# A four-batch attention, gated-FFN and scan kernel: layer-norm statistics of batches 1 to 3 in the pipeline fill, third loop iteration written out

## What is computed

```
x = x + attention(layernorm(x))     # 16 heads, low-rank q and kv, rotary part, causal softmax
x = x + ffn(layernorm(x))           # gate and up from a 16-entry table, silu, down
x = x + scan_layer(layernorm(x))    # projections, softplus decay, linear recurrence over tokens
x = x + ffn(layernorm(x))

def layernorm(x, eps=1e-5):
    m = mean(x, -1); v = var(x, -1)
    return (x - m) / sqrt(v + eps)
```

## Time and profile before

| | |
|---|---|
| median of 3 runs | 880.52 us (873.76 to 881.05) |
| the profiled execution | 879.84 us |
| its span, first to last instruction | 877.7 us |
| mean granted TensorE clock | 0.973 |
| busy: PE, DVE, ACT, POOL | 88%, 77%, 71%, 57% |

### The profile page before, as it was taken

The page is one execution under the profiler, slowest core; times in us unless marked ns, Lnnn a source line. Parts: engine busy times, 40 slices in busy tenths (PEclk is TensorE's granted clock), DMA queues, the critical chain, the costliest instruction groups (busy, mean ns, idle before and its releaser), DMA issues.

```text
span 877.7 us, 16980 instructions
## 1 busy us (share of the span) xinstructions
PE 771.6 (88%) x4556; PEld 657.8 (75%) x4556; DVE 673.6 (77%) x2210; ACT 624.7 (71%) x1532; POOL 502.4 (57%) x545
## 2 busy tenths in 40 slices
PE   4768989898887988977889899998798999999998
PEld 4656777777766877866777779876686887887887
DVE  3776898787789877879987789886666678777643
ACT  3457978898786988887889889998434666656232
POOL 1599999999999999999999999830000000000000
PEclk9788999999999999999999999999999999999999
DMA  9700000000000000000000010000000000000000
GB/s 238 250 1 1 1 1 2 1 2 1 4 2 1 1 1 2 1 5 2 0 1 1 2 38 1 1 1 1 1 1 1 1 1 1 1 1 24 26 25 24
DMA packets 15402, 14.78 MB, mean 17 GB/s; under 512 B 5793, under 2 KB 14433, under 8 KB 15041
## 3 DMA queue, kind: packets, MB, share of 16 engines
q1 hardware_dynamic: 13792, 11.41, 4.6%
q0 software_dynamic: 624, 2.12, 0.7%
q10 hardware_dynamic: 880, 0.04, 0.1%
HBM read 11.46 MB, written 2.10 MB: 15 GB/s over the span
## 4 chain that ended last, share of the span: by engine, by line
PE 50%; DVE 17%; issue 16%; ACT 15%; DVEq 1%; DMA 0%; ACTq 0%; SPq 0%
PE bank L562 10%; PE bank L564 10%; PE bank L563 10%; ACT prob L764 6%; PE bank L1371 4%; ACT prob L746 3%; ACT pt_hi L773 2%; DVE o_b L1067 2%; DVE bias_m L1020 2%; PE bank L1398 2%; PE bank L1400 2%; PE bank L1385 1%; PE bank L1388 1%; DVE q_tok L1034 1%; PE bank L1336 1%
## 5 line engine op out<-in xcount | busy, mean ns | idle before, releaser
L696 POOL TENSOR_SCALAR hot<-idx_gu,lut 128x256 f32<-128x256 bf16 x165 | 191.0, 1158 | 16.7
L746 ACT ACTIVATE prob<-bank,bias_m 128x128 f32<-128x128 f32 (+3 forms) x256 | 136.6, 534 | 27.6 <-DVE bias_m L1020 26.8
L1020 DVE CUSTOM_DVE_ANT_0 bank<-bank,mask 128x128 f32<-128x128 f32 (+3 forms) x256 | 126.3, 494 | 31.8 <-issue 30.7
L764 ACT ACTIVATE prob<-prob,rden 128x128 f32<-128x128 f32 (+3 forms) x256 | 128.0, 564 | 10.4 <-DVE rden L1052 6.2
L1061 DVE TENSOR_TENSOR pt_lo<-bank,pt_hi 128x512 fp32r<-128x512 f32 x160 | 109.3, 683 | 32.2 <-ACT pt_hi L773 32.1
L701 POOL TENSOR_TENSOR w_gu<-w_gu,hot 128x256 f32<-128x256 f32 x165 | 122.0, 739 | 13.8
L1371 PE MATMUL bank<-ident,prob 128*128 128x128 f32 x640 | 101.0, 281 | 24.6 <-ACT prob L764 17.3
L773 ACT CAST pt_hi<-bank 128x512 fp32r<-128x512 f32 x160 | 94.6, 591 | 20.0 <-PE bank L1371 13.9
L1371 PEld LDWEIGHTS bank<-ident,prob 128*128 128x128 f32 x640 | 74.3, 142 | 43.4 <-ACT prob L764 25.4
L696 POOL TENSOR_SCALAR hot<-idx_dn,lut 128x256 f32<-128x256 bf16 (+1 forms) x90 | 96.3, 1071 | 9.1
L562 PE MATMUL bank<-kt_hi,qt_hi 128*128 128x128 f32 (+3 forms) x256 | 89.6, 350 | 10.1 <-ACT kt_hi L739 4.3
(11 more groups left out here) (198 smaller groups left out, 2149.1 us busy)
## 6 DMA issues: line engine op xcount, KB each, us to landing
x<-in_L_attn_a_x_dram SPq DMA_DIRECT2D x4, 512.0 KB, 7.5
wo_nat<-in_L_attn_a_wo_dram SPq DMA_DIRECT2D x1, 2048.0 KB, 13.1
out_dram<-x SPq DMA_DIRECT2D x16, 128.0 KB, 1.7
wqu<-in_L_attn_a_wq_up_dram SPq DMA_DIRECT2D x2, 768.0 KB, 7.6
wqr<-in_L_attn_a_wq_rope_dram SPq DMA_DIRECT2D x4, 192.0 KB, 8.0
raw_dn<-in_L_ffn_down_idx_dram POOLq DMA_DIRECT2D x1, 688.0 KB, 10.4
raw_gu<-in_L_ffn_gate_idx_dram POOLq DMA_DIRECT2D x1, 640.0 KB, 7.7
raw_gu<-in_L_ffn_up_idx_dram POOLq DMA_DIRECT2D x1, 640.0 KB, 8.3
```

The lines of the kernel that those rows point to most:

```text
L696: nc.gpsimd.tensor_scalar(dst, idx[:, c:c + n], float(v), lut[:, v:v + 1], ALU.is_equal, ALU.mult).then_inc(lut_hot, 1)
L746: nc.scalar.activation(prob[:, n % 2, h, 0:w], bank[2 + h % 2][:, 0:w], ACT.Exp, bias=bias_m[:, n % 2, h:h + 1], scale=-1.0, accum_out=den ...
L764: nc.scalar.activation(prob[:, n % 2, h, 0:w], prob[:, n % 2, h, 0:w], ACT.Copy, scale=rden[:, n % 2, h:h + 1]).then_inc(norm_a, 1)
L1020: nc.vector.tensor_tensor_reduce(out=bank[2 + h % 2][:, 0:w], in0=bank[2 + h % 2][:, 0:w], in1=mask[:, TB * P - w:TB * P], scale=1.0, scal ...
```

## The change

Three things are done. (1) A new function at_stats_of computes statistics and reciprocal roots for a range of batches into tiles of their own (at_stats, at_mv, at_r); it is called for batch 0 at the start and for batches 1 to 3 at once behind fill slot 1, where only batch 1 was worked on. (2) In the loop body DVE's slots 8 and 9 keep only the four normalisations (at_norm), in the same four gaps of slot 9 as before. (3) The loop has 2 iterations; the third (b = 2) is written out on PE, ACT and DVE, and its layer norm of batch 0 for the FFN stays in slots 8 and 9 as it was. The wait for the loads of batches 2 and 3 moves ahead to fill slot 1.

```diff
+        def at_stats_of(b0, b1):
+            e, tiles = nc.vector, slice(b0 * TB, b1 * TB)
+            for t in range(b0 * TB, b1 * TB):
+                e.bn_stats(at_stats[:, t, :], x[:, t, :]).then_inc(at_bn, 1)
+            e.wait_ge(at_bn, b1 * TB)
+            settle(2 * G)
+            for t in range(b0 * TB, b1 * TB):
+                e.bn_aggr(at_mv[:, t, :], at_stats[:, t, :]).then_inc(at_agg, 1)
+            e.wait_ge(at_agg, b1 * TB)
+            c0 = 1 if b0 == 0 else RSQRT + 2
+            e.tensor_scalar(at_v[:, tiles], at_mv[:, tiles, 1], LN_EPS, None, ALU.add).then_inc(at_ref, 1)
+            for k in range(RSQRT):
+                rsqrt_step(k, at_ref, c0, at_v[:, tiles], at_r[:, tiles], at_t[:, tiles])
+
+        def at_norm(p, t):
+            e = nc.vector
+            free_after(e, xt_mm, 2 * p)
+            if t == 0:
+                e.wait_ge(at_ref, (RSQRT + 1) * (1 if isinstance(p, int) and p == 0 else 2))
+
+            def rows(m):
+                return m[:, bass.ds(p * TB + t, 1)]
+            e.tensor_scalar(xn[:, t, :], rows(x).rearrange("p a d -> p (a d)"), rows(at_mv)[:, :, 0], rows(at_r),
+                            ALU.subtract, ALU.mult).then_inc(ln_norm, 1)
+
         def ln_step(k, p, xb):
             e = nc.vector
 
             def rows(t):
                 return x[:, bass.ds(xb * TB + t, 1), :].rearrange("p a d -> p (a d)")
-            c0 = (RSQRT + 1) * p + 1
+            q = p - BATCH
+            c0 = (RSQRT + 1) * q + 1
             if k < TB:
                 e.bn_stats(stats[:, k, :], rows(k)).then_inc(ln_stats, 1)
             elif k == TB:
-                e.wait_ge(ln_stats, p * TB + TB)
+                e.wait_ge(ln_stats, q * TB + TB)
                 e.wait_ge(ln_norm, p * TB)
                 settle(2 * G)
                 for t in range(TB):
                     e.bn_aggr(mv[:, t, :], stats[:, t, :]).then_inc(ln_aggr, 1)
-                e.wait_ge(ln_aggr, p * TB + TB)
+                e.wait_ge(ln_aggr, q * TB + TB)
                 e.tensor_scalar(ln_v[:, :], mv[:, :, 1], LN_EPS, None, ALU.add).then_inc(ln_ref, 1)
             elif k <= TB + RSQRT:
                 rsqrt_step(k - TB - 1, ln_ref, c0, ln_v[:, :], ln_r[:, :], ln_t[:, :])
@@ -519,10 +551,6 @@
                 e.wait_ge(xt_mm, 2 * p)
                 e.tensor_scalar(xn[:, t, :], rows(t), mv[:, t, 0:1], ln_r[:, t:t + 1],
                                 ALU.subtract, ALU.mult).then_inc(ln_norm, 1)
-
-        def dve_ln(p, xb):
-            for k in range(LN_STEPS):
-                ln_step(k, p, xb)
...
@@ -833,9 +861,11 @@
                 act_tasks(act, *early_tasks(s))
                 if s == 3:
                     act_xt(1)
-            with act.Fori(0, BATCH - 1) as b:
+            with act.Fori(0, BATCH - 2) as b:
                 for s in range(LEAD, UNITS + LEAD):
                     act_slot(s, b, b + 1)
+            for s in range(LEAD, UNITS + LEAD):
+                act_slot(s, BATCH - 2, BATCH - 1)
             for s in range(LEAD, UNITS + DEPTH):
                 act_slot(s, BATCH - 1, None)
 
@@ -960,7 +990,9 @@
             prime(dve, "dve")
             nc.vector.memset(one[:, :], 1.0).then_inc(consts, 1)
             dve.wait_ge(x_in_s[0], 16)
-            dve_ln(0, 0)
+            at_stats_of(0, 1)
+            for t in range(TB):
+                at_norm(0, t)
             dve_xt(0)
             dve_tasks(dve, D0, N0)
 
@@ -1081,10 +1113,13 @@
 
                     if nb is None:
                         return
-                    if s in (8, 9):
+                    if not isinstance(nb, int):
+                        if s == 9 and 3 <= k < 3 + TB:
+                            at_norm(nb + 1, k - 3)
+                    elif s in (8, 9):
                         if s == 8 and k == 0:
 
-                            dve.wait_ge(x_add, 1 + b * TB)
+                            dve.wait_ge(x_add, 1 + TB)
                         ln_step(GAPS * (s - 8) + k, nb + 1, (nb + 1) % BATCH)
                     if s in (10, 11):
                         token_step(GAPS * (s - 10) + k, nb)
@@ -1146,15 +1181,18 @@
             for s in range(LEAD):
                 dve_slot(s, 0, None, early_tasks(s))
                 if s == 1:
-                    dve.wait_ge(x_in_s[1], 16)
-                    dve_ln(1, 1)
+                    for b in range(1, BATCH):
+                        dve.wait_ge(x_in_s[b], 16)
+                    at_stats_of(1, BATCH)
+                    for t in range(TB):
+                        at_norm(1, t)
                 if s == 3:
                     dve_xt(1)
-            for b in range(2, BATCH):
-                dve.wait_ge(x_in_s[b], 16)
-            with dve.Fori(0, BATCH - 1) as b:
+            with dve.Fori(0, BATCH - 2) as b:
                 for s in range(LEAD, UNITS + LEAD):
                     dve_slot(s, b, b + 1)
+            for s in range(LEAD, UNITS + LEAD):
+                dve_slot(s, BATCH - 2, BATCH - 1)
             for s in range(LEAD, UNITS + DEPTH):
                 dve_slot(s, BATCH - 1, None)
 
@@ -1475,9 +1513,11 @@
                 if s == 3:
                     pe.wait_ge(prep_dve, S0)
                     pe_xt(1)
-            with pe.Fori(0, BATCH - 1) as b:
+            with pe.Fori(0, BATCH - 2) as b:
                 for s in range(LEAD, UNITS + LEAD):
                     pe_slot(s, b, b + 1)
+            for s in range(LEAD, UNITS + LEAD):
+                pe_slot(s, BATCH - 2, BATCH - 1)
             for s in range(LEAD, UNITS + DEPTH):
                 pe_slot(s, BATCH - 1, None)
```

More of the change, by code:

```diff
@@ L120, in build @@
         rms_r = keep("rms_r", [P, TB * 2], F32)
+        at_stats = keep("at_stats", [P, BATCH * TB, 6], F32)
+        at_mv = keep("at_mv", [P, BATCH * TB, 2], F32)
+        at_v = keep("at_v", [P, BATCH * TB], F32)
+        at_t = keep("at_t", [P, BATCH * TB], F32)
+        at_r = keep("at_r", [P, BATCH * TB], F32)
         bias_m = keep("bias_m", [P, 2, G], F32)
@@ L217, in build @@
             sem(n) for n in ("ln_stats", "ln_aggr", "ln_ref", "ln_norm"))
+        at_bn, at_agg, at_ref = sem("at_bn"), sem("at_agg"), sem("at_ref")
         xt_mm, xt_hi_s, xt_lo_s = sem("xt_mm"), sem("xt_hi_s"), sem("xt_lo_s")
```

## The result

The changed kernel takes 870.33 us (median of 4 runs, 868.55 to 873.62) against 880.78 us (4 runs, 873.76 to 883.05). I had forecast 876.1 us in a range of 870 to 882.5, so the direction held and the size was too small by a factor of 2.6. Two executions of the experiments lay far above all others at a lower granted clock (the kernel before once at 908.4 us and 0.83, the changed kernel without GpSimd's work once at 1069.6 us and 0.65) and take no part in the ratios.

What follows compares the result with a forecast made beforehand. No engine was taken to bound the kernel alone, so an instruction is worth what it holds up in its slot. Terms +3.5 - 0.4 - 2.2 - 4.6 = -3.7 us, from 879.84 to 876.1 us; range 870 to 882.5 us.

Steps and rivals of the forecast that it cites:

- fill, from there to the first out_low: DVE's layer norm block behind fill slot 1: added statistics of further batches lie on the path in full, +3.5 us.
- head of iteration 0: First five slots of the loop body, iteration 0: removed DVE instructions save 0.4 us, bounds 0 and -2.8.
- head of iteration 1: Same five slots, iteration 1: return stays, slot 8 no longer delayed by statistics, -2.2 us, bounds -0.4 and -4.1.
- head of iteration 2: Same five slots, third iteration written out: no return to the loop's top, -4.6 us, bounds 0 and -6.
- the outermost bounds: Sums of the unknown terms' extremes: -9.4 us at one end, +4.1 at the other; the range was said to exclude both.
- Beyond that they are held by each other: Iteration 0, slot 8: PE waited only 0.40 us and ACT 0.56, otherwise each holds the other; so only -0.4 us.
- the mark that I had set as a sign of being wrong: Iteration 0: slot 8 shrinking by more than 1 us would show the prediction wrong.
- I take the third iteration to run as iteration 0 did: Third iteration's five-slot head, entered straight, takes 46.6 us like iteration 0 instead of 51.2: -4.6 us.
- constants for register counts: Written-out third iteration: constants might shorten slots 8 to 11 a little more, giving the bound of -6 us.
- The stall did not move: Rival: the written-out third iteration waits elsewhere as long as the return did; sum +0.9 us, 880.7 us; chance 0.13.
- DVE is the bound: Rival: DVE bounds slots 8 and 9, so removed time counts nearly in full; -8.0 us, 871.8 us; chance 0.12.
- The clock in the fill: Rival: longer PE idling in the fill prolongs half clock, costing up to 5 us; +1.3, 881.1 us; chance 0.08.

Runs made afterwards that it cites:

- quiet GpSimd: GpSimd's table work cut to one instruction per chunk, in four kernels: kernel before 862.65 us, third iteration written 857.02, fill only 867.20, all of the change 858.81.
- shifted: One more table instruction (1.16 us) on GpSimd ahead of its table work: kernel before 882.03 us; kernel before with only its third iteration written out 874.22 us.

## Why the prediction was right in its direction and too small

| term | forecast | changed kernel's trace | with a quiet GpSimd |
|---|---|---|---|
| up to batch 1's statistics (weights) | 0 | +0.3 (56.27 for 55.93) | -3.8 (53.80 for 57.55) |
| fill, from there to the first out_low | +3.5 | +3.3 (31.5 for 28.2) | +3.9 (29.8 for 25.9) |
| head of iteration 0 | -0.4 | -2.1 | -0.6 |
| head of iteration 1 | -2.2 | -2.7 | -1.4 |
| head of iteration 2 | -4.6 | -5.4 | -5.9 |
| all the rest | 0 | +0.7 | +1.4 |
| span | -3.7 | -5.9 | -6.4 |
| timed | -3.7 | -9.5 (-6.6 to -12.4) | -3.8 (-4.6 by ratios) |

**The forecast as a whole.** The median of 870.33 us lies 0.3 us inside the range's lower end. It misses the band of 872.5 to 879 that I had given 0.62, and it is faster by over 1%, which I had given 0.12 against 0.85 for a change within 1%. The prediction says that the range leaves out the outermost bounds; at the lower end that is wrong, since -9.4 us is 870.4 and the range begins at 870. That the time fell inside is luck in part: the range was wide because of the spread of the runs, not because a term was known to be larger.

**The fill** was right in mechanism and, within the 1.5 us that traces of one fill differ by, in size: all of the added work lay on the path, the block and the wait came out as 10.5 and 7.1 us, the loads were there, and bn_stats were not stretched.

**Iteration 0: the term was mis-sized, by a step that is missing.** "Beyond that they are held by each other" was right for slots 8 and 9: 18.9 us before, 18.5 in the changed kernel, and -0.6 in the quiet pair. The 1.0 us by which slot 8 alone shrank stands at the mark that I had set as a sign of being wrong; 0.6 us of it came back in slot 9. What I did not see is slot 10. The root steps of token_step there were stretched by GpSimd in all three iterations of before, by 1.4 to 1.7 us over the 12, and by 0.4 to 0.9 in the changed kernel. I had seen a stretched step in the fill, bounded its cost there, and did not ask the same of the loop. Why they met it less often afterwards is not settled. The removed statistics can't be the only reason, since the kernel with only the fill changed had slots 10 of 10.0 to 10.7 us too. In iteration 0 there is a pattern: slot 10 took 11.8 to 12.3 us in the four kernels with both the fill and the statistics of before, shifted or not, and 10.0 to 10.5 in the six in which either differs. It comes from one profiled execution each.

**Iteration 1** was near, -2.7 for -2.2, but by terms that cancel, which is luck. Its return cost 11.1 us of slot rather than 9.9, with the clock at 0.69 on average in that slot; slot 8 fell from 12.1 to 9.3 us, more than the 2.2 forecast, and slot 10 by 1.2 us, which was not in the sum. The mechanism named, late statistics behind DVE's own return, fits slot 8: without statistics it takes 9.2 or 9.3 us there in every kernel with a loop, and the quiet pair gives -1.7 us for it. The slot of the return itself took 8.8 to 11.3 us in iteration 1 over the kernels that have one, so part of this term was never to be had from one trace.

**Iteration 2: mis-sized, by 0.8 us.** The step "I take the third iteration to run as iteration 0 did" is what failed. Written out, it runs faster than iteration 0 did in the loop: 45.8 us for 46.6, and 42.0 for 42.9 with a quiet GpSimd. The second pair is the one that shows it: iteration 0's head of the same work took 42.7 to 43.0 us in three quiet kernels, but 45.9 to 47.2 in five with a busy GpSimd. I had kept this as a bound ("constants for register counts") and given it no value. Of the 5.4 us the entry slot gave 2.5, and slot 10, where the stretched steps are, 1.9.

**The rest.** In both columns one slot of the last batch took 8.3 us rather than 7.2, the clock falling to 1.2 GHz for a part of it; the changed kernel from 599 to 603 us:

```profile
599.00:603.00 4.00, 3.78 (x15) 3.29 (x16) 1.38 (x2) 2.18 (x5) 0.00 (x0) 0.57 0.00 0
```

**What stays open.** The timed gain is 9.5 us, its trace shows 5.9. Quiet, the two agree better: 3.8 us timed (4.6 by the ratios), and 2.6 by the trace if the 3.8 us ahead of the change's place are left out. The kernel with only its third iteration written shows the same: -8.4 timed, -5.6 timed when quiet, -5.4 in the slots of its trace. With GpSimd busy, then, the change seems to be worth some 5 us more than its own mechanisms, a surplus about as large as the intervals of the timings. Shifting GpSimd's start didn't take it away. The stretch of token_step's root steps differs in the traces in this direction (by 0.8 to 1.0 us an iteration), but one profiled execution a kernel, among runs that differ by 5 to 14 us, does not show where all of it lies.

**The rivals.** The stall did not move, as forecast: the third iteration's first slot took 5.8 us and no wait of a return's length came in its place; even with all iterations written the longest such wait of PE at the values matmul was 1.4 us. PE has one such wait of a return's length in the changed kernel (3.5 us), where it had two, and its wait for the rotary part in slot 8 of iteration 1 is gone. The rival "DVE is the bound" gave the better number (871.8 us) for a wrong reason in iteration 0: in slot 8 without statistics DVE is busy for 6.0 of 9.4 us and the slot still shortened by 1 us only. The clock in the fill did stay low for longer, 13.6 us (63.4 to 77.0 us) rather than 10.2, but the fill cost what its instructions cost. Whether the change made it longer isn't shown: in three other kernels with the fill of before and a busy GpSimd, the same stretch was 3.4, 6.8 and 7.0 us long.

## What to carry to other kernels

Price a removed instruction by what waits for it, then ask which shared resource the remaining ones meet: the same small step took 0.17 or 0.7 us here, depending on another engine's work. A loop return that costs 3 us on PE and 2 on DVE and ACT is worth finding with a stretch-by-stretch table, and the form without registers can be faster in itself. Work moved into the fill is cheap only in a hole of the engine that does it: moving it 7 us took 3.9 us from PE's wait, which is the 3.5 that the change had added and 0.4 of what stood there before. And a slot read from one execution can differ by 2 us from the next with the same work, so a difference of that size needs several traces or a timing.

## What the runs showed of the hardware

- A return to the loop's top left PE idle on "issue" for 2.9 to 3.5 us, DVE for 2.0 to 2.1 and ACT for 1.8 to 1.9 in the kernels before and after (PE up to 3.9, ACT up to 2.6 in the experiments); leaving the loop into written-out code showed no such gap, and with all iterations written out the longest of PE's at that matmul was 1.4 us.
- DVE's root steps on 4 to 12 columns took 0.14 to 0.17 us with GpSimd idle and up to 0.72 us with it busy; bn_stats kept a pitch of 0.33 us in a block, and 0.41 us each in the loop, in both. GpSimd's table work, never waited for in attention, cost the whole kernel 18.4 us.
- The same instructions in slot 8 took 10.1 us in the loop and 9.3 us written out, with GpSimd idle.
